# Another order of a pair's jobs on all four engines of an attention and expert kernel

## The chip, the cores and the metric

One core of a Trainium2 chip runs the whole program. The metric is the device time of one execution in microseconds. Three executions of the kernel before took 3823.05, 3824.71 and 3825.47 us; the median is 3824.71 us. Five engines work side by side, each through its own list of instructions in program order, and wait for one another by semaphores: TensorE (PE, with its weight loads PEld), VectorE (DVE), ScalarE (ACT), GpSimd (POOL) and SyncE (SP), which here issues the DMAs.

## The reference

The input x is [8, 512, 256]. After a layer norm two branches are computed and both are added to x.

```python
xn = _layernorm(x, axis=-1)
# branch 1: causal attention, 16 heads of 16
score = einsum('bhqd,bhkd->bhqk', Q, K) / sqrt(16) + causal mask
out1 = (softmax(score) @ V) @ WO
# branch 2: 16 heads of 64, experts E = 8 with the best 2 kept
q = _rope(einsum('bsd,hdp->bhsp', x, Wq));  k = _rope(einsum('bsd,hdp->bhsp', x, Wk))
gv = _gate(x, Wsel_v);  go = _gate(x, Wsel_o)          # sigmoid, top 2 of 8
v = einsum('bsd,bhse,hedp->bhsp', x, gv, Wv)
o = einsum('bhst,bhtp->bhsp', softmax(q k / 8), v)
src2 = einsum('bhsp,bhse,hepd->bsd', o, go, Wo)
src = _ln(src + src2);  out2 = _ln(src + relu(src @ W1 + b1) @ W2 + b2)
return x + out1 + out2
```

## The kernel before

The program has three stages. The first (about 230 us) normalizes the eight batches, computes the gates and stores them. The second, about 3300 us, goes over 64 pairs: a pair is one batch and two neighbouring heads of both branches, with the weights of two heads kept for eight batches in a row. The third (from about 3540 us) does the feed-forward part, the norms and the sum.

A pass of the loop over pairs works on three pairs at once: it computes the attention scores of pair `it` in eight steps, prepares pair `it + 1` (projections, values, rotated heads) and finishes pair `it - 1` (attend, expert products). Even steps handle a 128-row block of the two big heads, odd steps one of the causal heads. Per step TensorE computes the scores of the next step into two banks (L718, or L723 and L724), then the jobs that a table names for this step, then the transposes of this step's exponentials (L748). VectorE takes the row maxima (L1184), ScalarE the exponentials (L1016) and later copies the transposes out (L1030).

The tables are `PE_FILL`, `ACT_FILL`, `DVE_FILL` and `POOL_FILL`, one list of jobs per step, written out by hand. There is no scheduler: each engine's order is the order of its table, and every wait is computed from the tables. The jobs:

- R, AT, AC: transposed reciprocals (L793), attend (L811) and causal attend (L821) of the pair before; ON on VectorE normalizes the result (L1232).
- U, UH, UL, J, one for each of eight experts: VectorE multiplies the attended heads with an expert's gate (`uf`, L1239), ScalarE copies the high part (`u_h`, L1062), GpSimd subtracts for the low part (`u_l`, L569), TensorE multiplies with the expert's weights (L836) into two banks that collect all eight. Both `uf`, `u_h` and `u_l` have two buffers: U waits for the UL two before it, UH for the J two before it.
- P, four projections of the next pair (L705 with `wq_h`); ScalarE copies each to `raw` (L1044).
- V, eight value tiles (L705 with `wv_h`); VectorE multiplies by the gates and adds up (L1206, L1208).
- RP, RS, PA, PB, VN, SQ, SK on GpSimd: rotation of the heads and splitting of the causal heads into stacked bf16 parts (L580 to L608). VC and VA copy the values for attend (L560, L565). RD widens reciprocals (L574).
- QK, two groups of head transposes (L775); QH and QL make the high and low parts `q_h`, `k_h` (L1047, ScalarE) and `q_l`, `k_l` (L1218, L1220, VectorE). ST and SO: stack transposes (L784) and their copies (L1050).

AT, AC, P, V and QK write to two banks in turn, in the order of the PE table. A job waits until the reader of the bank's last content has freed it: P2 for the raw copy of P0, V6 for q_l of the first head transposes. That rule is these lines:

```python
W_JOBS = {k: [j for j in fills(k, PE_FILL) if j[0] in ("AT", "AC", "P", "V", "QK")] for k in range(5)}
```

A pass of the loop on TensorE is:

```python
if s < SLOTS - 1:
    scores(s + 1, it)
elif kind != LAST:
    heads_ready()
    scores(0, n)
for job in fill(kind, PE_FILL, s):
    do(job)
turn(s)
```

Scores wait until the exponentials of the step before have been taken from their banks. SyncE loads gates, inputs and weights; its waits are on the fourth and eighth U and on V3 and V7.

Of the kernel before, what the change touches and what calls it, by code (L numbers as in the profile page):

```python
# [9 lines left out]
P, E = 64, 8  # L10
# [24 lines left out]
AHEAD = ("P", "V", "QK", "ST", "QH", "QL", "SO", "RP", "RS", "PA", "PB", "VN", "SQ", "SK")  # L35

PE_FILL = [[("R", 0), ("AT", 0), ("AC", 0)],
           [("P", 0), ("P", 1), ("P", 2), ("P", 3)],
           [("J", 0), ("V", 0), ("V", 1)],
           [("J", 1), ("V", 2), ("J", 2)],  # L40
           [("V", 3), ("J", 3), ("V", 4)],
           [("J", 4), ("V", 5), ("J", 5)],
           [("QK", 0), ("QK", 1), ("V", 6), ("J", 6)],
           [("ST", 0), ("ST", 1), ("V", 7), ("J", 7)]]
ACT_FILL = [[("AT", 0), ("AC", 0)],
            [("UH", 0), ("P", 0), ("P", 1), ("UH", 1), ("P", 2), ("P", 3)],
            [("UH", 2)],
            [("UH", 3)],
            [("UH", 4), ("UH", 5)],
            [("UH", 6)],  # L50
            [("QH", 0), ("QH", 1), ("UH", 7)],
            [("SO", 0), ("SO", 1)]]
DVE_FILL = [[("ON", 0), ("U", 0)],
            [("U", 1)],
            [("V", 0), ("U", 2), ("V", 1)],
            [("V", 2), ("U", 3)],
            [("V", 3), ("U", 4), ("U", 5), ("V", 4)],
            [("V", 5), ("U", 6)],
            [("QL", 0), ("QL", 1), ("U", 7), ("V", 6), ("RECIP", 0)],
            [("V", 7), ("YA", 0)]]  # L60
POOL_FILL = [[],
             [("VC", 0), ("VA", 0), ("UL", 0), ("UL", 1)],
             [("RP", 0), ("UL", 2)],
             [("RS", 0), ("UL", 3), ("PA", 0)],
             [("PB", 0), ("UL", 4), ("UL", 5)],
             [("SQ", 0), ("UL", 6)],
             [("VN", 0), ("SK", 0), ("UL", 7)],
             [("RD", 0)]]
V_ORDER = [(0, 0), (0, 1), (1, 0), (1, 1), (0, 2), (0, 3), (1, 2), (1, 3)]

# [10 lines left out]
def fill(kind, table, s):  # L81

    return [j for j in table[s] if present(kind, j)]


def fills(kind, table):

    return [j for s in range(SLOTS) for j in fill(kind, table, s)]
# [42 lines left out]
def build(nc, x, wqk, wv, wo, wsel, w_out, w1, w2, b1, rows, ident, ident_h, mask, rope, rank, out):  # L131
# [12 lines left out]
    with ExitStack() as ctx:  # L144
# [819 lines left out]
        def _(act):  # L964
# [45 lines left out]
            def exps(s, n):  # L1010

                qt, w = s // 2, S if s % 2 == 0 else (s // 2 + 1) * NP
                for j in range(2):
                    act.wait_ge(nmax_ready, n * UNITS + 2 * s + j + 1)
                    kw = {"accum_out": den[:, qt, j:j + 1]} if s % 2 == 0 else {}
                    nc.scalar.activation(probs[:, s % 2, j, 0:w], sbank[j][:, 0:w], ACT.Exp, bias=nmax[:, 2 * s + j:2 * s + j + 1], **kw).then_inc(exp_done, 1)  # L1016

            def body(kind, it):
# [19 lines left out]
                def do(job):  # L1038
                    name, i = job
                    if name == "P":  # L1040
                        o, free = w_filled(job)
                        if i == 0 and kind != PRO:
                            act.wait_ge(stack_ready, n)
                        nc.scalar.activation(raw[:, i, :], o[:, 0:NPROJ], ACT.Copy).then_inc(free, 1)  # L1044
                    elif name == "QH":
                        o, _ = w_filled(("QK", i))
                        nc.scalar.activation((q_h, k_h)[i][:], o[:], ACT.Copy, scale=(P ** -0.5, 1.0)[i]).then_inc(qk_high, 1)  # L1047
                    elif name == "SO":
                        act.wait_ge(t_full[i], t_at(kind, it, i, ("ST", i)) + 1)
                        nc.scalar.activation(stackT[:, 2 * i:2 * i + 2, :], tbank[i].bitcast(bf16)[0:STK, :].rearrange("q (g s) -> q g s", g=2),  # L1050
                                             ACT.Copy, scale=(CA ** -0.5, 1.0)[i]).then_inc(t_free[i], 1)
                    elif name == "AT":
                        o, free = w_filled(job)
                        nc.scalar.activation(oo[:, 0], o[:], ACT.Copy).then_inc(free, 1)
                    elif name == "AC":
                        o, free = w_filled(job)
                        act.wait_ge(a_stored, 64 * of + 16)
                        nc.scalar.activation(a_out[:], o[0:2 * STRIP, :], ACT.Copy).then_inc(free, 1)
                    else:
                        act.wait_ge(u_ready, of * E + i + 1)  # L1060
                        act.wait_ge(o_done, of * E + i - 1) if kind == TAIL or i > 1 else None
                        nc.scalar.activation(u_h[:, i % 2], uf[:, i % 2], ACT.Copy).then_inc(uh_done, 1)  # L1062

                if kind in (PRO, TAIL):
                    for job in fills(kind, ACT_FILL):
                        do(job)
# [3 lines left out]
                for s in range(SLOTS):  # L1070
                    if s < SLOTS - 1:
                        exps(s + 1, it)
                    elif kind != LAST:
                        exps(0, n)
                    for job in fill(kind, ACT_FILL, s):
                        do(job)
# [29 lines left out]
        def _(dve):  # L1106
# [72 lines left out]
            def row_max(s, n):  # L1179

                w = S if s % 2 == 0 else (s // 2 + 1) * NP
                for j in range(2):
                    dve.wait_ge(s_full, n * UNITS + 2 * s + j + 1)
                    nc.vector.tensor_reduce(nmax[:, 2 * s + j:2 * s + j + 1], sbank[j][:, 0:w], AX.X, ALU.max, negate=True).then_inc(nmax_ready, 1)  # L1184

            def body(kind, it):
# [61 lines left out]
                if kind in (PRO, TAIL):  # L1248
                    for job in fills(kind, DVE_FILL):
                        do(job)  # L1250
# [3 lines left out]
                for s in range(SLOTS):  # L1254
                    if s < SLOTS - 1:
                        row_max(s + 1, it)
                    elif kind != LAST:
                        row_max(0, n)
                    for job in fill(kind, DVE_FILL, s):
                        do(job)  # L1260
# [100 lines left out]
```

## Time and profile before

| what | value |
|---|---|
| median of 3 executions | 3824.71 us |
| the profiled execution's own time | 3826.32 us |
| its span, first to last instruction | 3824.5 us |
| busy: TensorE, VectorE, ScalarE, GpSimd | 3358.3, 2142.5, 1823.2, 1722.9 us |
| mean granted TensorE clock | 0.97 of 2.4 GHz |
| moved by DMA | 265.57 MB, 69 GB/s over the span |

Busy time of one engine overlaps that of the others, so the shares don't add up. A row of the timeline gives the start of a group of like instructions, its length, and in square brackets how long the engine had been idle before it and whose work ended the idle time. The chain of waits follows the work that ended last back from step to step; a row there gives start, length and what ran. In a row "x6" is the count of instructions.

### The profile page before, as it was taken

The page shows a single profiled execution, that of the slowest core. Times are in us where ns is not written, and L with a number is a line of the kernel's source. Part 1 is how long each engine was busy: PE and PEld are TensorE (multiplying, and loading weights), DVE is VectorE, ACT ScalarE, POOL GpSimd, SP SyncE. Part 2 cuts the span into 40 slices and gives each one's busy share as a digit, 9 for nine tenths or more (in the row PEclk, how much of TensorE's full clock was granted, in tenths as well). Part 3 has the DMA queues.
Part 4 walks back from the last instruction along what each step waited for, and adds up shares of the span by engine and source line. Part 5 has one row for each costly group of instructions (what it writes and reads, how often), then busy time and mean ns, then how long its engine had stood idle before and what let it go on. Part 6 is the DMA issues. An engine that isn't in the chain of part 4 may idle for free.

```text
span 3824.5 us, 63063 instructions
## 1 busy us (share of the span) xinstructions
PE 3358.3 (88%) x18656; PEld 2456.8 (64%) x18656; DVE 2142.5 (56%) x3602; ACT 1823.2 (48%) x3906; POOL 1722.9 (45%) x1911
## 2 busy tenths in 40 slices
PE   2259999999999999999999999999999999998998
PEld 1246666666666666666666666666666666665666
DVE  6765555555555555555555555555555555555553
ACT  2235555555555555555555555555555555554211
POOL 2124445544554455444554465445544455444122
PEclk7679999999999999999999999999999999999999
DMA  3122233222322232223222322222322222223121
GB/s 107 62 87 54 55 83 79 67 63 56 94 59 60 68 82 79 61 58 82 63 68 68 82 77 53 68 61 74 79 68 67 74 71 68 55 65 91 58 66 44
DMA packets 88947, 265.57 MB, mean 69 GB/s; under 512 B 28240, under 2 KB 40784, under 8 KB 72272
## 3 DMA queue, kind: packets, MB, share of 16 engines
q1 hardware_dynamic: 88912, 265.15, 26.5%
q8 instruction: 17, 0.28, 0.0%
q14 instruction: 18, 0.15, 0.0%
HBM read 243.61 MB, written 21.50 MB: 69 GB/s over the span
## 4 chain that ended last, share of the span: by engine, by line
PE 57%; issue 19%; DVE 10%; POOL 8%; ACT 6%; ACTq 0%; DMA 0%; POOLq 0%; SPq 0%; DVEq 0%
PE bank L705 14%; PE bank L836 10%; PE bank L748 6%; PE bank L811 6%; PE bank L718 5%; PE bank L821 4%; PE bank L944 4%; PE bank L936 3%; POOL u_l L569 3%; PE bank L784 2%; ACT raw L1044 1%; ACT pt_c L1030 1%; DVE vm L1206 1%; ACT probs L1016 1%; DVE nmax L1184 1%
## 5 line engine op out<-in xcount | busy, mean ns | idle before, releaser
L569 POOL TENSOR_TENSOR u_l<-uf,u_h 128x512 fp32r<-128x512 f32 x512 | 653.2, 1287 | 1009.6 <-ACT u_h L1062 1009.5
L705 PE MATMUL bank<-wv_h,xx 128*128 128x512 f32 x2048 | 738.3, 407 | 153.2 <-DVE q_l L1218 153.2
L1184 DVE TENSOR_REDUCE nmax<-bank 128x1 f32<-128x512 f32 (+3 forms) x1024 | 556.3, 585 | 518.3 <-PE bank L724 267.4
L1062 ACT ACTIVATE u_h<-uf 128x512 fp32r<-128x512 f32 x512 | 323.7, 633 | 824.7 <-DVE uf L1239 815.3
L1016 ACT ACTIVATE probs<-bank,nmax 128x512 f32<-128x512 f32 (+3 forms) x1024 | 590.5, 607 | 222.3 <-DVE nmax L1184 219.3
L1206 DVE TENSOR_TENSOR vm<-bank,gv 128x512 f32<-128x512 f32 x512 | 353.7, 691 | 536.8 <-PE bank L705 536.8
L705 PEld LDWEIGHTS bank<-wv_h,xx 128*128 128x128 f32 x2048 | 390.5, 191 | 254.9 <-DVE q_l L1218 168.4
L836 PE MATMUL bank<-u_h,wo_h 128*128 128x512 f32 x1024 | 427.5, 417 | 39.3 <-POOL u_l L569 34.2
L748 PE MATMUL bank<-ident_sb,probs 128*128 128x128 f32 x3328 | 456.0, 275 | 0.9 <-ACT stackT L1050 0.9
L748 PEld LDWEIGHTS bank<-ident_sb,probs 128*128 128x128 f32 x3328 | 389.4, 141 | 73.8 <-issue 13.3
L705 PE MATMUL bank<-wv_l,xx 128*128 128x512 f32 x1024 | 406.6, 397 | 0.0
L1239 DVE TENSOR_TENSOR uf<-oo,go 128x512 f32<-128x512 f32 x512 | 396.1, 783 | 17.3 <-POOL u_l L569 8.0
L836 PE MATMUL bank<-u_h,wo_l 128*128 128x512 f32 x1024 | 404.8, 395 | 0.0
L836 PE MATMUL bank<-u_l,wo_h 128*128 128x512 f32 x1024 | 403.5, 394 | 0.0
L1208 DVE TENSOR_REDUCE v_next<-vm 128x64 f32<-128x512 f32 x512 | 351.4, 686 | 17.5
L705 PE MATMUL bank<-wq_h,xx 128*128 128x352 f32 x1024 | 282.3, 338 | 69.6 <-ACT raw L1044 63.3
L1030 ACT ACTIVATE pt_e<-bank 128x512 f32<-128x512 f32 x512 | 275.5, 589 | 126.9 <-PE bank L748 126.7
L560 POOL TENSOR_TENSOR v_sb<-v_next,zero_hb 128x512 f32<-128x512 f32 x64 | 76.6, 1196 | 494.0 <-PE bank L811 488.9
L836 PEld LDWEIGHTS bank<-u_h,wo_h 128*128 128x128 f32 x1024 | 193.9, 189 | 147.7 <-issue 86.2
L705 PEld LDWEIGHTS bank<-wq_h,xx 128*128 128x128 f32 x1024 | 183.5, 190 | 111.0 <-ACT raw L1044 81.5
L811 PE MATMUL bank<-pt_e,v_sb 128*64 128x512 f32 x1024 | 233.8, 598 | 0.0
L836 PEld LDWEIGHTS bank<-u_h,wo_l 128*128 128x128 f32 x1024 | 192.7, 188 | 45.0
(141 smaller groups left out, 5012.0 us busy)
## 6 DMA issues: line engine op xcount, KB each, us to landing
go<-go_d SPq DMA_DIRECT2D x256, 512.0 KB, 6.2
xx<-xs_d SPq DMA_DIRECT2D x128, 512.0 KB, 3.6
pt_c<-in_x SPq DMA_DIRECT2D x16, 512.0 KB, 4.6
st<-in_wv SPq DMA_DIRECT2D x16, 512.0 KB, 6.6
xs_d<-xx SPq DMA_DIRECT2D x8, 1024.0 KB, 4.1
st<-in_wo SPq DMA_DIRECT2D x16, 512.0 KB, 7.4
a_d<-a_out SPq DMA_DIRECT2D x128, 32.0 KB
uf<-a_d SPq DMA_DIRECT2D x16, 256.0 KB
```

What stands on the lines that cost most here:

```text
L569: nc.gpsimd.tensor_tensor(u_l[:, e % 2], uf[:, e % 2], u_h.bitcast(f32)[:, e % 2], ALU.subtract).then_inc(ul_done, 1)
L705: last = nc.tensor.matmul(out, lhs, rhs, start=n == 1, stop=n == 3 * len(chunks))
L748: mm = nc.tensor.transpose(o[:, c * NP:(c + 1) * NP], probs[:, s % 2, j, c * NP:(c + 1) * NP], ident_sb[:])
L811: mm = nc.tensor.matmul(o[j * P:(j + 1) * P, :], v_sb[:, k, j, :], pt_e[:, j, k, :], start=k == 0, stop=k == TT - 1)
L836: mm = nc.tensor.matmul(ybank[i][:], w[:, e, c], u[:, e % 2], start=e == 0 and k == 0, stop=e == E - 1 and k == 2, skip_group_check=True)
L1016: nc.scalar.activation(probs[:, s % 2, j, 0:w], sbank[j][:, 0:w], ACT.Exp, bias=nmax[:, 2 * s + j:2 * s + j + 1], **kw).then_inc(exp_done, 1)
L1030: nc.scalar.activation(dst[:, j, 0:m, qt * NP:(qt + 1) * NP], tbank[j][:, 0:m * NP].rearrange("q (c m) -> q c m", m=NP), ACT.Copy).then_in ...
L1062: nc.scalar.activation(u_h[:, i % 2], uf[:, i % 2], ACT.Copy).then_inc(uh_done, 1)
L1184: nc.vector.tensor_reduce(nmax[:, 2 * s + j:2 * s + j + 1], sbank[j][:, 0:w], AX.X, ALU.max, negate=True).then_inc(nmax_ready, 1)
L1206: nc.vector.tensor_tensor(m, o[:].rearrange("q (c e) -> q c e", e=E), g, ALU.mult).then_inc(free, 1)
L1208: nc.vector.tensor_reduce(v_next[:, t, j, :], m, AX.X, ALU.add).then_inc(v_ready, 1)
L1239: nc.vector.tensor_tensor(uf[:, i % 2], oo[:, 1], go[:, i], ALU.mult).then_inc(u_ready, 1)
```

## The change

The four tables are rewritten; nothing else is. Each job is done as often as before, by the same engine, with the same waits. Three things move. The first expert product stands between the projections P1 and P2 (the first two `u_h` and U come in the first step for it), and from there expert products and value tiles alternate. The two head transposes stand at the end of the sixth step instead of the start of the seventh, with QH and QL to match, and UH and U of the eighth expert come ahead of them. On GpSimd and VectorE u work comes a little earlier among the other jobs. The steps are counted from one.

```diff
 PE_FILL = [[("R", 0), ("AT", 0), ("AC", 0)],
-           [("P", 0), ("P", 1), ("P", 2), ("P", 3)],
-           [("J", 0), ("V", 0), ("V", 1)],
-           [("J", 1), ("V", 2), ("J", 2)],
-           [("V", 3), ("J", 3), ("V", 4)],
-           [("J", 4), ("V", 5), ("J", 5)],
-           [("QK", 0), ("QK", 1), ("V", 6), ("J", 6)],
+           [("P", 0), ("P", 1), ("J", 0), ("P", 2), ("P", 3)],
+           [("V", 0), ("J", 1), ("V", 1)],
+           [("V", 2), ("J", 2), ("V", 3)],
+           [("J", 3), ("V", 4), ("J", 4)],
+           [("V", 5), ("J", 5), ("QK", 0), ("QK", 1)],
+           [("J", 6), ("V", 6)],
            [("ST", 0), ("ST", 1), ("V", 7), ("J", 7)]]
-ACT_FILL = [[("AT", 0), ("AC", 0)],
-            [("UH", 0), ("P", 0), ("P", 1), ("UH", 1), ("P", 2), ("P", 3)],
-            [("UH", 2)],
+ACT_FILL = [[("AT", 0), ("AC", 0), ("UH", 0), ("UH", 1)],
+            [("P", 0), ("P", 1), ("UH", 2), ("P", 2), ("P", 3)],
             [("UH", 3)],
-            [("UH", 4), ("UH", 5)],
-            [("UH", 6)],
-            [("QH", 0), ("QH", 1), ("UH", 7)],
+            [("UH", 4)],
+            [("UH", 5), ("UH", 6)],
+            [("UH", 7), ("QH", 0), ("QH", 1)],
+            [],
             [("SO", 0), ("SO", 1)]]
-DVE_FILL = [[("ON", 0), ("U", 0)],
-            [("U", 1)],
-            [("V", 0), ("U", 2), ("V", 1)],
-            [("V", 2), ("U", 3)],
-            [("V", 3), ("U", 4), ("U", 5), ("V", 4)],
-            [("V", 5), ("U", 6)],
-            [("QL", 0), ("QL", 1), ("U", 7), ("V", 6), ("RECIP", 0)],
+DVE_FILL = [[("ON", 0), ("U", 0), ("U", 1)],
+            [("U", 2)],
+            [("V", 0), ("U", 3), ("V", 1)],
+            [("V", 2), ("U", 4), ("V", 3)],
+            [("U", 5), ("V", 4), ("U", 6)],
+            [("V", 5), ("U", 7), ("QL", 0), ("QL", 1)],
+            [("V", 6), ("RECIP", 0)],
             [("V", 7), ("YA", 0)]]
 POOL_FILL = [[],
              [("VC", 0), ("VA", 0), ("UL", 0), ("UL", 1)],
-             [("RP", 0), ("UL", 2)],
-             [("RS", 0), ("UL", 3), ("PA", 0)],
-             [("PB", 0), ("UL", 4), ("UL", 5)],
-             [("SQ", 0), ("UL", 6)],
-             [("VN", 0), ("SK", 0), ("UL", 7)],
+             [("UL", 2), ("RP", 0), ("UL", 3)],
+             [("RS", 0), ("UL", 4)],
+             [("PA", 0), ("UL", 5), ("PB", 0)],
+             [("UL", 6), ("SQ", 0)],
+             [("UL", 7), ("VN", 0), ("SK", 0)],
              [("RD", 0)]]
```

Below are two places in the instruction lists, in program order without times. REGISTER_ALU and ISA rows only prepare or hold a wait.

On TensorE, second step of a pass, between the second projection and the third (L705 with wq), the difference of the two orders:

```order
 L705 MATMUL bank<-wq_l,xx 128x352
 L705 MATMUL bank<-wq_h,xx 128x352
+L827 ISA
+L832 ISA
+L836 MATMUL bank<-u_h,wo_h 128x512
+L836 MATMUL bank<-u_l,wo_h 128x512
+L836 MATMUL bank<-u_h,wo_l 128x512
+L836 MATMUL bank<-u_h,wo_h 128x512
+L836 MATMUL bank<-u_l,wo_h 128x512
+L836 MATMUL bank<-u_h,wo_l 128x512
 L734 REGISTER_ALU
 L705 MATMUL bank<-wq_h,xx 128x352
```

The six matmuls of the first expert product (L836) now stand between the two projections; they stood behind the next scores.

On TensorE, before, the head transposes (L775) and what stands on either side: scores of the causal heads ahead, the value tile V6 and an expert product behind.

```order
L723 MATMUL bank<-stackT 128x512
L724 MATMUL bank<-mask_sb,ident_hb 128x128
L734 REGISTER_ALU
L773 REGISTER_ALU
L775 MATMUL bank<-ident_sb,raw 128x128 x8
L734 REGISTER_ALU
L705 MATMUL bank<-wv_h,xx 128x512
L705 MATMUL bank<-wv_l,xx 128x512
L705 MATMUL bank<-wv_h,xx 128x512 x2
L705 MATMUL bank<-wv_l,xx 128x512
L705 MATMUL bank<-wv_h,xx 128x512
```

The same place on TensorE in the changed kernel, from the head transposes on:

```order
L775 MATMUL bank<-ident_sb,raw 128x128 x8
L739 REGISTER_ALU
L746 REGISTER_ALU
L748 MATMUL bank<-ident_sb,probs 128x128 x3
L739 REGISTER_ALU
L748 MATMUL bank<-ident_sb,probs 128x128 x3
L712 REGISTER_ALU
L723 MATMUL bank<-stackT 128x512
L724 MATMUL bank<-mask_sb,ident_hb 128x128
L723 MATMUL bank<-stackT 128x512
L724 MATMUL bank<-mask_sb,ident_hb 128x128
L827 REGISTER_ALU
```

Behind the last row come the six matmuls of the seventh expert product and only then V6: six transposes, the scores and a product now lie between the head transposes and the tile that reuses their bank.

On ScalarE, before, around the copies of the turned heads (q_h, k_h):

```order
L1030 ACTIVATE pt_c<-bank 128x3x128
L1029 REGISTER_ALU
L1030 ACTIVATE pt_c<-bank 128x3x128
L1016 ACTIVATE probs<-bank,nmax 128x512 x2
L1035 REGISTER_ALU
L1047 ACTIVATE q_h<-bank 128x512
L1035 REGISTER_ALU
L1047 ACTIVATE k_h<-bank 128x512
L1060 REGISTER_ALU
L1062 ACTIVATE u_h<-uf 128x512
```

And in the changed kernel:

```order
L1062 ACTIVATE u_h<-uf 128x512
L1035 REGISTER_ALU
L1047 ACTIVATE q_h<-bank 128x512
L1035 REGISTER_ALU
L1047 ACTIVATE k_h<-bank 128x512
L1029 REGISTER_ALU
L1030 ACTIVATE pt_c<-bank 128x3x128
L1029 REGISTER_ALU
L1030 ACTIVATE pt_c<-bank 128x3x128
L1016 ACTIVATE probs<-bank,nmax 128x512 x2
```

q_h and k_h have moved ahead of the pt_c copies and the exponentials of the eighth step, and the last u_h has moved ahead of q_h.

## Rows read from the trace of the kernel before

**Rows 1.** The page, busy time of each engine over the span.
```profile
PE 3358.3 (88%) x18656; PEld 2456.8 (64%) x18656; DVE 2142.5 (56%) x3602; ACT 1823.2 (48%) x3906; POOL 1722.9 (45%) x1911
```

**Rows 2.** Waits of TensorE, 400 to 3400 us: total us, times, longest.
```profile
PE bank L705 <- DVE q_l L1218: 140.4, 58, 2.4
PE bank L705 <- ACT raw L1044: 59.9, 59, 1.0
PE bank L836 <- POOL u_l L569: 29.8, 59, 0.5
```

**Rows 3.** Chain of waits, pieces in order: start us, us, what.
```profile
298.10 3.58 PE bank L811 x16
...
1527.69 3.58 PE bank L811 x16
...
1556.14 1.39 PE bank L705 x6
...
1568.15 1.65 PE bank L705 x6
...
1578.66 1.43 PE bank L811 x5
...
3473.79 3.58 PE bank L811 x16
```

**Rows 4.** Chain of waits in another pair, 590 to 612 us.
```profile
595.28 2.93 PE bank L705 x6
```

**Rows 5.** Windows: us, busy of PE, PEld, DVE, ACT, POOL; clock, DMA share, GB/s.
```profile
1527.70:1578.70 51.00, 47.02 (x274) 34.55 (x276) 28.52 (x47) 26.70 (x59) 25.83 (x30) 1.00 0.26 63
595.00:598.50 3.50, 3.22 (x8) 2.60 (x9) 1.68 (x4) 0.63 (x1) 1.34 (x2) 0.55 0.27 89
3560.00:3800.00 240.00, 239.18 (x923) 165.78 (x922) 125.96 (x329) 49.38 (x86) 51.19 (x21) 1.00 0.19 60
```

**Rows 6.** Timeline of TensorE in one pair, around its three waits.
```profile
1537.29 0.32 PE L705 MATMUL bank<-wq_h,xx 128*128 128x352 f32 x1
1538.60 0.43 PE L705 MATMUL bank<-wq_h,xx 128*128 128x352 f32 x1 [1.00 <-ACT raw L1044]
...
1554.52 0.47 PE L836 MATMUL bank<-u_h,wo_h 128*128 128x512 f32 x1 [0.51 <-POOL u_l L569]
...
1564.70 1.04 PE L775 MATMUL bank<-ident_sb,raw 128*128 128x128 f32 x8
1568.15 0.50 PE L705 MATMUL bank<-wv_h,xx 128*128 128x512 f32 x1 [2.41 <-DVE q_l L1218]
```

**Rows 7.** Timeline of ScalarE in the same pair.
```profile
1534.28 1.06 ACT L1030 ACTIVATE pt_e<-bank 128x512 f32<-128x512 f32 x2
1538.09 0.81 ACT L1044 ACTIVATE raw<-bank 128x352 f32<-128x352 f32 x2
...
1566.76 0.61 ACT L1047 ACTIVATE q_h<-bank 128x512 fp32r<-128x512 f32 x1
```

**Rows 8.** Timeline of VectorE in the same pair.
```profile
1532.89 0.69 DVE L1239 TENSOR_TENSOR uf<-oo,go 128x512 f32<-128x512 f32 x1
...
1556.23 1.16 DVE L1239 TENSOR_TENSOR uf<-oo,go 128x512 f32<-128x512 f32 x1
...
1562.30 0.69 DVE L1206 TENSOR_TENSOR vm<-bank,gv 128x512 f32<-128x512 f32 x1 [1.67 <-PE bank L705]
...
1563.63 0.68 DVE L1239 TENSOR_TENSOR uf<-oo,go 128x512 f32<-128x512 f32 x1
...
1567.41 0.69 DVE L1218 SCALAR_TENSOR_TENSOR q_l<-bank,q_h 128x512 fp32r<-128x512 f32 x1 [1.50 <-ACT q_h L1047]
```

**Rows 9.** Timeline of GpSimd in the same pair.
```profile
1533.72 0.43 POOL L565 TENSOR_TENSOR va<-va_next,zero_hb 128x128 f32<-128x128 f32 x1 [1.11 <-PE bank L821]
...
1547.18 1.29 POOL L569 TENSOR_TENSOR u_l<-uf,u_h 128x512 fp32r<-128x512 f32 x1 [2.89 <-ACT u_h L1062]
...
1555.83 1.01 POOL L594 TENSOR_TENSOR part<-rot,zero_hb 128x256 bf16<-128x256 f32 x1
```

## The prediction

> **What bounds the kernel now.** I read the page first: TensorE is busy 88% of the span, VectorE 56%, the others under 50% [rows 1]. So TensorE sets the pace, and the question is what stands in its idle time. The list of waits gives that for the long loop over pairs: between 400 and 3400 us, in 59 pairs, it waits 140.4 us for q_l of VectorE, 59.9 us for the copy raw of ScalarE and 29.8 us for u_l of GpSimd, and for nothing else [rows 2]. The chain of waits gives a pair's length: the attend product starts at 298.10 and 3473.79 us with 62 pairs between, and from 1527.69 to the next at 1578.66 in an ordinary one, 50.97 us [rows 3]. In that pair TensorE is busy 47.0 of 51.0 us [rows 5]. About 4 us of each pair can be won, and no more, as no product is removed.
>
> Some pairs are longer. In one of them the value tile behind the q_l wait takes 2.93 us instead of 1.65, and the granted clock around it is 0.55, so part of it ran at the lower level of 1.2 GHz [rows 3 to 5]; the chain has nine such rows in the loop, 1.28 us each. With 3175.69 us for the 62 pairs and 62 times 50.97 being 3160.1, 15.6 us remain, of which they are 11.5.
>
> **What each wait really costs.** The idle time is counted from a matmul's end, which lies behind its issue, and the first matmul after a wait takes longer to make room. By starts [rows 6]: eight head transposes start at 1564.70 and take 0.96 us to issue, the value product behind them starts at 1568.15, so 2.49 us; its first start-to-start is 0.34 and not 0.23, so 2.6. The second projection's last matmul starts at 1537.29 and the third projection at 1538.60; a matmul of that size takes 0.16 to issue, so 1.15, with its slow first 1.26. Before the fourth expert product at 1554.52 the idle time shown is 0.51; with the same 0.16 and the slow first it is 0.75. Together 4.6 us a pair, of which 3.9 show as idle.
>
> **The change, part by part.** Nothing is added or removed on any engine; the order alone moves. I follow one pair with the old durations, time 0 being the start of the attend product. Issue times on TensorE [rows 3, 6]: attend 3.58, causal attend until 5.9 (its reader starts at 6.03, [rows 9]), value tile 1.39 and expert product the same (six matmuls of 512 columns both), projection 6 times 0.16 and its start, 1.02, eight transposes 0.96, even scores 0.9, odd ones 0.3 to 0.56. I add 0.1 for an expert product that follows scores.
> New order: causal 3.6, transposes 5.9, scores 6.8, projections P0 7.7 and P1 8.7, product J0 9.8, P2 11.25, P3 12.3, value V0 13.8, J1 15.2, V1 16.6, V2 19.9, J2 21.3, V3 22.7, J3 25.0, V4 26.5, J4 27.9, V5 31.1, J5 32.5, head transposes 33.9, scores 35.5, J6 36.1, V6 37.6, transposes 39.0, next scores 39.9, stack transposes 40.8, V7 41.7, J7 43.2, next attend 46.5.
> Now each thing that could be late.
>
> First product before P2. On ScalarE the first two u_h copies now stand ahead of the pt_e copies, which started at 6.6 [rows 7]; uf is written at 5.2 to 5.9 and the next behind it [rows 8], so the copies run 6.6 to 7.6 and pt_e to 8.7. GpSimd has va until 6.5 [rows 9], then u_l in 1.29 us [rows 9] from 7.2: done at 8.5, where J0 wants it at 9.8. Cost nothing; the cover is P0 and P1. The exponentials slip from 8.5 to 8.75, and the raw copy of P0, which waited behind them and one u_h and started at 10.4 [rows 7], starts at 10.1 and ends at 10.6. P2 wants that at 11.25: the 1.15 us wait goes, because J0's 1.4 us stand where it was. Slack 0.65 us.
>
> Expert products alternate with value tiles. u is now one step further ahead: with the waits in force (a u needs the u_l two before it, a u_h the product two before it) u_l of J1 is done at 9.8 (wanted 15.2), of J2 at 13.4 (21.3), of J3 at 19.5 (25.0), of J4 at 25.5 (27.9), of J5 at 29.3 (32.5), of J6 at 32.6 (36.1), of J7 at 36.8 (43.2). The 0.68 us wait goes, the nearest next one has 2.4 us left.
>
> Head transposes at the end of the sixth step. They need the rotation, done near 21, and the banks of V4 and V5, the latter free at 33.4 for a second group that starts at 34.4. Behind them stand six transposes, the scores and J6, together 2.7 us of work where there was none. The chain to V6 is: V5 done on TensorE, its two VectorE passes (1.33 from the first to the u behind them), u 0.69, a copy 0.53 from start to start, q_h 0.61, q_l 0.69 [rows 7, 8]: q_l ends at 36.7, V6 wants it at 37.6. Slack 0.9 us, though U7 and its copy are now ahead of q_h and q_l. k_l and the row maxima follow, the exponentials end at 39.2, the next scores want them at 39.9. Slack 0.7 us, the tightest but one. On GpSimd the stack copies end near 38.5, wanted at 40.8.
>
> Queues. SyncE's order is unchanged; its loads wait for the fourth and eighth u and for V3 and V7, which all come earlier in the pair, and their data are wanted half a pair later. Once per eight pairs GpSimd splits the next value weights at the end of a pair: two halves of two passes over 1024 elements, each at most twice the 1.29 us of u_l's 512 [rows 9]. From 42.7 on that is 10.3 us, until 6.5 of the next pair; v_sb, another 1.3, and va 0.43 follow, u_l then ends at 9.5. J0 still wants it at 9.8: cost nothing, with 0.3 us to spare.
>
> **GpSimd and VectorE together.** A u took 1.16 us instead of 0.68 beside GpSimd's part split, and the split itself took 1.0 [rows 8, 9]. In the new order the third and the seventh u lie beside GpSimd work. I took 0.4 us more for each; their u_l have over 3 us left, so this costs 0. The least is 0, the most is all eight u's at 0.48, 3.8 us on VectorE, which has 22 us idle in a pair: it would eat the 0.7 and 0.9 us slacks and add under 1 us a pair. I take 0, since the row shows it for two u's of eight.
>
> **Sum.** A pair is shorter by 4.6 less 0.15 for the new starts behind a wait, 4.45 us; 62 pairs give 276 us. The slow clock comes right behind the 2.4 us wait, which goes: 12 us more. The first pair (without products, its waits partly stay) gives 1 us, a guess; the last pair and the closing stage are taken as they are. 289 us from the profiled execution's own 3826.3 us leave 3537 us. The median shown is 1.6 us below the own time, less than the estimate's error; I stay at 3537. The bounds of this case: if all 4.6 us and the whole 15.6 us go, 3826 less 301, so 3525; if only the idle seen is won, 3.92 by 62, and the clock dips stay, 3583.
>
> **Rivals.**
> (A) The clock dips stay. They cost 1.28 us in nine of the pairs. For it: transposes and short scores still stand in a row in steps six and seven. Against: the dips I see all begin at the matmul after the 2.4 us idle, and between 3560 and 3800 us TensorE is busy 239 of 240 us at clock 1.00 [rows 5]. Time 3537 plus 12, so 3549. The Trainium skill (TensorE: Matmul & The Clock Gate, Part 4: PE-mode transpose) says that transposes do not count as busy for the clock gate as other matmuls do; by that rule 14 transposes in a row could be read as a pause. The rows at 595 us show a dip behind transposes and a wait together, so they do not separate the two.
> (B) A new wait takes part of the gain. The three tight places are P2 on raw (0.65 us left), V6 on q_l (0.9) and the scores on the exponentials (0.7); all hang on ScalarE doing in order what it did later before. One being 1 to 2 us later than I put it costs 0.3 to 1.3 us in each of 62 pairs: 19 to 80 us, middle 50, so 3587. For it: four engines in fixed order, and the contention above. Against: each chain is short and made of durations that hardly vary.
> (C) Slower than before: U7 and its copy stand ahead of q_h on ScalarE and q_l on VectorE, and U7 waits for the sixth u_l. A u_l later than 34.1, where U7 could start, holds up V6, all that follows and the next pair. The sixth u_l, at 29.3 in my walk, would have to be 4.8 us late to show, 0.9 more to reach V6 and another 4.45 to make the pair longer than before: it decides from 10.2 us late. At 12 us late a pair is 1.8 us longer and the kernel takes 3826 plus 112, 3938. Against: nothing in GpSimd's queue before it is 10 us long; it has 25.8 us of work in the pair [rows 5].
> (D) The waits change names and the pair stays at 51 us: 3825. It would take a wait outside TensorE's banks, and none of the other engines is over 29 us busy in a pair [rows 5].
>
> **Chances.** Forecast 0.66, (A) 0.09, (B) 0.20, (C) 0.03, (D) 0.02. A difference of 0.2%, about 8 us, is what a measurement can tell here. Faster: 0.95; within: 0.02; slower: 0.03. The forecast's own range is 3522 to 3583; with (A) inside it and most of (B), 3520 to 3605 leaves out about 0.15.
>
> **What would show it.** In the new profile: attend to attend 46.4 to 46.7 us; TensorE busy 94% or more; no wait for q_l or raw, none for u_l above 0.3 us; the third projection starting right behind a product; the granted clock without single dips in the loop; the raw copy of the first projection ending before the first expert product does. If the pair is 47 to 48 us, the wait that ends last in it, before P2, V6 or the scores, names which slack I got wrong. If all 62 are 46.5 us and the time still misses, the first or last pairs or the closing stage moved, which I left alone.

## The result: 8.1% faster, and beyond the forecast's range

The changed kernel takes 3513.02 us (median of 4, 3512.62 to 3513.2) against 3825.04 us (3823.05 to 3825.47). The ratio is 0.9186, 95% interval 0.9175 to 0.9198. I had forecast 3537 us with a range of 3520 to 3605: the direction and the mechanism held, the gain of 312 us is 24 us more than I gave, and 7 us beyond the range's lower end.

Page of the changed kernel, busy time of each engine, answers to [rows 1]:

```profile
PE 3296.6 (94%) x18656; PEld 2453.1 (70%) x18656; DVE 2160.5 (62%) x3602; ACT 1841.1 (52%) x3906; POOL 1728.1 (49%) x1911
```

TensorE does the same 18656 matmuls in 62 us less busy time (less low clock, and no matmul that runs out ahead of a wait or starts slowly behind one) and stands idle 252 us less. The list of TensorE's waits between 400 and 3100 us, which had three rows in [rows 2], is empty. The window there (columns as in [rows 5]):

```profile
400.00:3100.00 2700.00, 2696.61 (x15842) 2018.06 (x15841) 1680.72 (x2683) 1567.89 (x3377) 1497.68 (x1703) 1.00 0.30 77
```

3.4 us idle in 2700. The loop is bound by TensorE's own work now. The attend products in the chain of waits, first, two in the middle, last two:

```profile
292.12 3.58 PE bank L811 x16
...
1496.86 3.58 PE bank L811 x16
1543.21 3.58 PE bank L811 x16
...
3164.72 3.58 PE bank L811 x16
3194.69 3.61 PE bank L811 x16
```

62 pairs take 2872.60 us, 46.33 each, against 3175.69 [rows 3]. Every pair is between 46.3 and 46.4 us. So the 313.7 us by which the span is shorter are: 303.1 in the 62 pairs, 6.0 ahead of the first attend product (298.10 to 292.12), 6.0 in the last pair (35.98 to 29.97), and 1.4 lost behind it.

TensorE's timeline of one pair at the three former waits, answers to [rows 6]:

```profile
1506.46 0.33 PE L705 MATMUL bank<-wq_h,xx 128*128 128x352 f32 x1
1506.62 0.40 PE L836 MATMUL bank<-u_h,wo_h 128*128 128x512 f32 x1
...
1508.02 0.32 PE L705 MATMUL bank<-wq_h,xx 128*128 128x352 f32 x1
...
1530.66 1.04 PE L775 MATMUL bank<-ident_sb,raw 128*128 128x128 f32 x8
...
1534.19 0.39 PE L705 MATMUL bank<-wv_h,xx 128*128 128x512 f32 x1
```

No row has a bracket with idle time, and the third projection's first matmul takes 0.32 instead of 0.43. The other engines in the same pair (ScalarE, then VectorE, then GpSimd), answers to [rows 7 to 9]:

```profile
1506.77 0.81 ACT L1044 ACTIVATE raw<-bank 128x352 f32<-128x352 f32 x2
...
1532.05 0.58 ACT L1047 ACTIVATE q_h<-bank 128x512 fp32r<-128x512 f32 x1
```

```profile
1505.88 1.36 DVE L1239 TENSOR_TENSOR uf<-oo,go 128x512 f32<-128x512 f32 x1
...
1532.65 0.69 DVE L1218 SCALAR_TENSOR_TENSOR q_l<-bank,q_h 128x512 fp32r<-128x512 f32 x1 [1.18 <-ACT q_h L1047]
```

```profile
1502.90 0.75 POOL L565 TENSOR_TENSOR va<-va_next,zero_hb 128x128 f32<-128x128 f32 x1 [1.11 <-PE bank L821]
1504.15 2.54 POOL L569 TENSOR_TENSOR u_l<-uf,u_h 128x512 fp32r<-128x512 f32 x2 [0.50 <-ACT u_h L1062]
```

q_l ends at 1533.34 (1532.65 and 0.69), V6 starts at 1534.19: 0.85 us of slack, where the walk had 0.9. The first of the two raw copies ends near 1507.2 (one takes 0.47), the third projection starts at 1508.02: 0.8, where it had 0.65. Counted from the attend product's first matmul at 1496.79, J0 stands at 9.8 and V6 at 37.4 us; the walk had 9.8 and 37.6.

### The profile page after: what moved, and what is told of

Same layout as the page of the kernel before. It is cut to its first block, busy times and chain, and to the rows that moved or that the text cites. A ratio compares the mean times of both kernels' runs of the same rounds, so it can differ in the third digit from the quotient of the medians.

```text
span 3510.8 us, 63063 instructions
## 1 busy us (share of the span) xinstructions
PE 3296.6 (94%) x18656; PEld 2453.1 (70%) x18656; DVE 2160.5 (62%) x3602; ACT 1841.1 (52%) x3906; POOL 1728.1 (49%) x1911
## 4 chain that ended last, share of the span: by engine, by line
PE 93%; DVE 5%; issue 1%; ACT 1%; DMA 0%; POOL 0%; SPq 0%; POOLq 0%; DVEq 0%; ACTq 0%
PE bank L705 28%; PE bank L836 20%; PE bank L748 11%; PE bank L811 7%; PE bank L718 7%; PE bank L821 4%; PE bank L944 4%; PE bank L936 3%; PE bank L723 2%; PE bank L784 2%; PE bank L775 2%; PE bank L679 1%; PE bank L724 1%; PE bank L793 1%; DVE pt_e L1161 1%
## 5 line engine op out<-in xcount | busy, mean ns | idle before, releaser
L705 PE MATMUL bank<-wv_h,xx 128*128 128x512 f32 x2048 | 743.3, 404 | 0.7 <-DVE q_l L1218 0.7
L1062 ACT ACTIVATE u_h<-uf 128x512 fp32r<-128x512 f32 x512 | 316.4, 629 | 531.2 <-DVE uf L1239 480.0
L705 PEld LDWEIGHTS bank<-wv_h,xx 128*128 128x128 f32 x2048 | 384.7, 188 | 125.5 <-issue 46.2
L1239 DVE TENSOR_TENSOR uf<-oo,go 128x512 f32<-128x512 f32 x512 | 414.8, 821 | 17.8 <-POOL u_l L569 8.5
L836 PE MATMUL bank<-u_h,wo_h 128*128 128x512 f32 x1024 | 414.8, 405 | 5.4 <-ACT u_h L1062 2.6
L836 PE MATMUL bank<-u_h,wo_l 128*128 128x512 f32 x1024 | 405.0, 396 | 0.0
L836 PE MATMUL bank<-u_l,wo_h 128*128 128x512 f32 x1024 | 403.4, 394 | 0.0
L705 PE MATMUL bank<-wv_l,xx 128*128 128x512 f32 x1024 | 401.4, 392 | 0.0
L705 PE MATMUL bank<-wq_h,xx 128*128 128x352 f32 x1024 | 275.6, 332 | 6.1 <-DMA xx<-xs_d 6.1
L836 PEld LDWEIGHTS bank<-u_h,wo_h 128*128 128x128 f32 x1024 | 192.8, 188 | 55.2 <-issue 5.2
L836 PEld LDWEIGHTS bank<-u_h,wo_l 128*128 128x128 f32 x1024 | 192.4, 188 | 44.6
L836 PEld LDWEIGHTS bank<-u_l,wo_h 128*128 128x128 f32 x1024 | 193.2, 189 | 37.0
```

The lines of the kernel that those rows point to most:

```text
L705: last = nc.tensor.matmul(out, lhs, rhs, start=n == 1, stop=n == 3 * len(chunks))
L836: mm = nc.tensor.matmul(ybank[i][:], w[:, e, c], u[:, e % 2], start=e == 0 and k == 0, stop=e == E - 1 and k == 2, skip_group_check=True)
L1239: nc.vector.tensor_tensor(uf[:, i % 2], oo[:, 1], go[:, i], ALU.mult).then_inc(u_ready, 1)
```

## Experiments

Two theories stood at the start. W: each of the three waits has its price in issue gaps (2.6, 1.26 and 0.75 us a pair), and the prices add up. I: a wait is worth only the idle time that the list shows. After the first runs a third question took over, about the low clock.

**One part at a time, from the kernel before.**

j0_only:
```diff
-           [("P", 0), ("P", 1), ("P", 2), ("P", 3)],
-           [("J", 0), ("V", 0), ("V", 1)],
+           [("P", 0), ("P", 1), ("J", 0), ("P", 2), ("P", 3)],
+           [("V", 0), ("V", 1)],
...
-ACT_FILL = [[("AT", 0), ("AC", 0)],
-            [("UH", 0), ("P", 0), ("P", 1), ("UH", 1), ("P", 2), ("P", 3)],
+ACT_FILL = [[("AT", 0), ("AC", 0), ("UH", 0)],
+            [("P", 0), ("P", 1), ("UH", 1), ("P", 2), ("P", 3)],
```


> The kernel before with one thing changed: the first expert product stands between the second and the third projection (its u_h comes in the first step for it). Theory W (each of TensorE's three waits costs the gap between the issues around it plus the slow first matmul, 1.26 us here): a pair 49.71 us, 78 us less in 62 pairs, 3747 us; the wait for raw is gone, q_l and u_l waits stay, and so do the single slow-clock intervals behind the q_l wait. Rival I (a wait costs only the idle time the list of waits shows, 1.00 us here, and the rest of the gain came from elsewhere): 3763 us. Rival S (the parts only work together): the raw wait comes back in another place and the time stays at 3825 us.

Measured 3822.08 us, ratio 0.9995 (0.9984 to 1.0006): nothing. Waits of TensorE between 450 and 3100 us:

```profile
PE bank L705 <- DVE q_l L1218: 125.7, 52, 2.4
PE bank L836 <- POOL u_l L569: 26.3, 52, 0.5
```

The raw wait is gone as W says. But the chain of waits shows this in two pairs that follow each other, and 61 of the 62 pairs are like them:

```profile
1524.41 3.58 PE bank L811 x16
...
1563.59 2.93 PE bank L705 x6
1575.59 3.58 PE bank L811 x16
...
1614.80 2.92 PE bank L705 x6
```

The value tile behind the q_l wait takes 2.93 us, the low clock's length of [rows 4], in all pairs but one. In the kernel before it was ten of the 62, not nine as I had counted: the first pair of the loop has a low interval too (52.62 us long). A pair is 51.18 us, the one clean pair 49.76. All three theories missed that: W's 1.26 us were won (50.97 to 49.76) and 1.4 us of low clock came in for them. The window from 450 to 3100 us shows a granted clock of 0.97, where the kernel before has 0.99:

```profile
450.00:3100.00 2650.00, 2496.73 (x14073) 1844.28 (x14070) 1474.01 (x2380) 1378.28 (x3003) 1336.71 (x1520) 0.97 0.27 70
```

The last pair fell from 35.98 to 32.20 us by this part alone.

heads_only:
```diff
-           [("J", 4), ("V", 5), ("J", 5)],
-           [("QK", 0), ("QK", 1), ("V", 6), ("J", 6)],
+           [("J", 4), ("V", 5), ("J", 5), ("QK", 0), ("QK", 1)],
+           [("V", 6), ("J", 6)],
...
-            [("UH", 6)],
-            [("QH", 0), ("QH", 1), ("UH", 7)],
+            [("UH", 6), ("QH", 0), ("QH", 1)],
+            [("UH", 7)],
```
(QL and U7 on VectorE likewise.)

> The kernel before with one thing changed: the two head transposes end the sixth step, with their q_h, k_h and q_l, k_l copies; V6 stands before J6 as it did. Six transposes and the scores, 1.2 us, now cover part of the wait. Theory W: q_h still follows the seventh u_h, so 0.3 to 0.5 us of idle time stays for q_l; the pair 48.9 us, 127 us less plus 12 us for the slow-clock intervals that go: 3686 us. Rival I: only 2.0 us less idle, 3701 us, slow-clock intervals in the loop as before. Rival S: 3825 us.

Measured 3692.03 us, 0.9655 (0.9627 to 0.9683). The q_l wait falls to 0.5 us a pair and the loop has no low interval; a pair is 49.09 us. That is 6 us above W: the wait left is at the top of what I gave, and the pair 0.2 us longer than W had. The first attend product starts 4 us earlier than before, which hides part of that.

swap_only:
```diff
-           [("QK", 0), ("QK", 1), ("V", 6), ("J", 6)],
+           [("QK", 0), ("QK", 1), ("J", 6), ("V", 6)],
```


> The kernel before with one thing changed: in the seventh step the expert product J6 stands before the value tile V6, which waits for q_l. Theory W: V6 starts when q_l ends as before, and J6's 1.4 us are done by then, so the pair is 1.4 us shorter, 86 us; the idle in one piece falls from 2.4 to under 1 us. If the slow clock follows that idle, its intervals go too: 3727 us. Rival C (the slow clock follows the row of transposes and short matmuls, not the idle time): they stay, 3739 us. Rival S: the u_l of J6 becomes the wait and nothing is won, 3825 us.

Measured 3727.82 us, 0.9748 (0.972 to 0.9777), and no low interval in the loop: W within 1 us. The 62 pairs gave 96.1 of W's 98 us; that the total fits closer is chance, since the first projection started 2.1 us earlier in this run. One swapped entry of one table is worth 97 us. What is left of the long wait is 0.7 us of idle time in front of J6 (for u_l) and 0.2 us in front of V6. The transposes and scores stand in a row as before, which speaks against rival C.

alternation_only:
```diff
-           [("J", 0), ("V", 0), ("V", 1)],
-           [("J", 1), ("V", 2), ("J", 2)],
-           [("V", 3), ("J", 3), ("V", 4)],
-           [("J", 4), ("V", 5), ("J", 5)],
+           [("J", 0), ("V", 0), ("J", 1), ("V", 1)],
+           [("V", 2), ("J", 2), ("V", 3)],
+           [("J", 3), ("V", 4), ("J", 4)],
+           [("V", 5), ("J", 5)],
```
(U and UH of the middle steps move to match; GpSimd's table is the one of the change.)

> The changed kernel with the first expert product put back behind the fourth projection and the head transposes back in the seventh step: only the alternation of expert products and value tiles, and u earlier, are left of the change. Theory W: the u_l wait (0.75 us) goes, q_l and raw waits stay: 50.2 us a pair, 46 us less, 3779 us; slow-clock intervals stay. Rival I: 0.51 us a pair, 3793 us. In the last pair, where TensorE waits for the expert chain, this part alone gives up to the 6 us that the whole change gave there (theory); the rival is that those 6 us came with the first product.

Measured 3824.48 us, 1.0001 (0.999 to 1.0012): nothing again, though the u_l wait is gone. From the chain of waits, three pairs, the first two with a slow value tile, the third without:

```profile
913.45 3.58 PE bank L811 x16
...
952.99 2.91 PE bank L705 x6
965.05 3.58 PE bank L811 x16
...
1004.52 2.92 PE bank L705 x6
1016.43 3.58 PE bank L811 x16
...
1066.44 3.58 PE bank L811 x15
```

51.60, 51.38 and 50.01 us. Of 62 pairs 48 are above 51.3 and 14 near 50.0 or 50.3. A clean pair is 0.7 to 1.0 us shorter than the 50.97 before, so W's 0.75 was there, and the low clock took it. The last pair did not gain here (37.48 us), as the rival has it. Of the last pair's 6.0 us, j0_only alone gives 3.8.

**Is it the idle time that brings the low clock?** j0_only is the place to ask, since it has it in every pair. Two kernels fill the wait for q_l with work that is thrown away:

```diff
                         turn_heads(i)
+                        if i == 1 and kind == INNER:
+                            o = t_bank(0, ("turn", 6))
+                            for m in range(20):
+                                nc.tensor.transpose(o[:, (m % 4) * NP:(m % 4 + 1) * NP], ident_sb[:], ident_sb[:])
```
(fill_transposes; fill_matmuls has nine matmuls of `xx` with `wv_h` in their place.)

> j0_only (the kernel before with the first expert product between the second and third projection, 51.2 us a pair, the low clock level in every pair) with nine more matmuls of 512 columns behind the head transposes, 2.2 us of work into a transpose bank that is overwritten later; their result is not used. V6 still waits for q_l, so they take no time of their own. Theory (the low level follows the idle time in front of V6): no low intervals, 49.8 us a pair, 87 us less than j0_only, 3735 us. Rival (the low level comes with the pair's length or with the row of transposes and scores before the wait, whatever fills it): 3822 us or more.

> As fill_matmuls, but the 2.2 us are filled with twenty transposes of 128 columns, whose result is not used. Theory (idle time alone counts, transposes are work like any other): as fill_matmuls, 3735 us and no low intervals. Rival (transposes do not count as work for the clock, which is what the Trainium skill says in TensorE: Matmul & The Clock Gate, Part 4: PE-mode transpose): low intervals as in j0_only, 3822 us.

Measured 3728.06 us (0.9747, 0.9718 to 0.9775) and 3727.07 us (0.9744, 0.9716 to 0.9772). Both are 94 and 95 us faster than j0_only, with more work per pair. The timeline of fill_transposes at the place:

```profile
1524.80 1.04 PE L775 MATMUL bank<-ident_sb,raw 128*128 128x128 f32 x8
1525.68 2.35 PE L851 MATMUL bank<-ident_sb 128*128 128x128 f32 x20
1528.25 0.50 PE L705 MATMUL bank<-wv_h,xx 128*128 128x512 f32 x1 [0.23 <-DVE q_l L1222]
```

V6 waits for q_l still, 0.23 us. No pair has the low clock: all 62 are between 49.6 and 49.9 us, in both kernels, and the window shows 1.00 where j0_only had 0.97:

```profile
450.00:3100.00 2650.00, 2608.63 (x15575) 1956.96 (x15572) 1520.65 (x2452) 1421.78 (x3097) 1383.52 (x1565) 1.00 0.28 72
```

A clean pair of j0_only was as long (49.76 us), and the transposes and scores ahead of the wait are the same. So the low clock needs the idle time, here 2.4 us; the pair's length or what stands before the wait do not bring it by themselves. And the twenty float32 transposes kept the clock high as well as the nine matmuls did. The rule of the Trainium skill (TensorE: Matmul & The Clock Gate, Part 4: PE-mode transpose) that transposes do not count the same way is not borne out at this place; the trace calls them MATMUL like all others and doesn't show which mode they ran in. This is the one experiment that shows directly that the low clock needs the idle time.

**One part undone, from the changed kernel.**

heads_back:
```diff
-           [("V", 5), ("J", 5), ("QK", 0), ("QK", 1)],
-           [("J", 6), ("V", 6)],
+           [("V", 5), ("J", 5)],
+           [("QK", 0), ("QK", 1), ("V", 6), ("J", 6)],
...
-            [("UH", 7), ("QH", 0), ("QH", 1)],
             [],
+            [("QH", 0), ("QH", 1), ("UH", 7)],
```
(QL and U7 on VectorE likewise.)

> The changed kernel with one thing undone: the head transposes and their copies are back in the seventh step, V6 ahead of J6. Theory W: TensorE waits 2.4 us for q_l again, 2.6 us a pair, 48.9 us, plus 161 us: 3674 us where the clock stays high. Theory L (learned from the first four runs: with the q_l wait in place the low clock level comes in many pairs and costs 1.4 us each, and how many depends on where the wait falls): between 3674 and 3761 us, with low intervals in the loop. Rival: without the other two waits the low level stays rare as in the kernel before: 3674 to 3685 us.

Measured 3715.95 us, 0.9717 (0.9698 to 0.9737). Waits of TensorE, 450 to 3100 us, and the window:

```profile
PE bank L705 <- DVE q_l L1218: 114.3, 53, 2.2
```

```profile
450.00:3100.00 2650.00, 2530.60 (x14560) 1881.21 (x14558) 1556.46 (x2463) 1444.97 (x3106) 1390.78 (x1570) 0.98 0.28 72
```

31 of the 62 pairs are 48.6 to 49.0 us and 31 are 50.2 to 50.5. In 29 of the long ones the record of the granted clock has a low interval, so nearly every second pair; the other two, the 7th and the 15th, have none, and TensorE stands idle 1.2 us ahead of an expert product there, which no other pair shows and which I did not follow up. That is theory L, whose range was wide (87 us); W and the rival lie 31 to 42 us too low. The head transposes' place is worth 203 us beside the other parts, against 133 us alone, and some 45 us of that are the low clock's (29 times 1.54, the difference of the two kinds of pair).

j0_back, then j0_back2, which also moves the third u_h:
```diff
-           [("P", 0), ("P", 1), ("J", 0), ("P", 2), ("P", 3)],
-           [("V", 0), ("J", 1), ("V", 1)],
+           [("P", 0), ("P", 1), ("P", 2), ("P", 3)],
+           [("J", 0), ("V", 0), ("J", 1), ("V", 1)],
...
-            [("P", 0), ("P", 1), ("UH", 2), ("P", 2), ("P", 3)],
-            [("UH", 3)],
+            [("P", 0), ("P", 1), ("P", 2), ("P", 3)],
+            [("UH", 2), ("UH", 3)],
```
(The first hunk is j0_back, both are j0_back2.)

> The changed kernel with one thing undone: the first expert product stands behind the fourth projection again (ahead of V0), the u_h copies stay early. Theory W: the copy raw of the first projection ends at 10.45 us after the attend product's start, the third projection wants it at 9.8: 0.6 us idle, 0.75 us in all, pair 47.1 us, 3559 us, clock high throughout. Rival I: 0.6 us a pair, 3550 us. Rival C (any wait behind a row of products brings the low level back): above 3590 us.

> As j0_back, with the third u_h moved behind the raw copies of the third and fourth projection on ScalarE too, where j0_back left it ahead of them and so made V0 wait for the first expert product. Theory W: one wait of 0.6 us is left, ahead of the third projection, 0.75 us in all: 47.1 us a pair, 3559 us. Rival: both waits come from the place of the product itself and the pair stays at 48.5 us, 3653 us.

j0_back measured 3652.67 us, 0.9552 (0.9533 to 0.9571), 94 us above what W said. The clock is high throughout; TensorE waits twice a pair:

```profile
PE bank L705 <- ACT raw L1044: 92.8, 109, 1.1
```

109 times in 55 pairs: 0.5 us ahead of the third projection and 1.1 us ahead of the value tile V0. The third u_h waits for the first product, which now stands behind the fourth projection, and it is ahead of the raw copies of the third and fourth projection on ScalarE. So those copies come late, and V0, which writes to the third projection's bank, waits. My edit had moved only one of two places that belong together. j0_back2 measured 3567.41 us, 0.9327 (0.9299 to 0.9354), one wait a pair (31.7 us, 56 times), most pairs 47.1 us. W to 8 us. Seven pairs, every eighth, are 47.6 us. heads_only, swap_only and j0_back have such a pair 0.2 to 0.4 us longer every eighth time too, the changed kernel has none. Weights are kept for eight pairs in a row, so their split is the likely cause; no run tests it.

v6_first:
```diff
-           [("J", 6), ("V", 6)],
+           [("V", 6), ("J", 6)],
```


> The changed kernel with V6 ahead of J6 in the seventh step. q_l ends 36.55 us after the attend product's start; V6 would start at 35.9. Theory W: 0.65 us idle and a slow first matmul, 0.75 us a pair, 46 us, 3559 us, clock high. Rival (J6's place is free, as q_l has 0.85 us of slack): 3513 us.

Measured 3555.37 us, 0.9295 (0.9268 to 0.9322), a wait for q_l of 0.5 us, a pair of 47.02. J6's place is worth 42 us beside the other parts.

**How much room is left on the path to V6.** delay1 and delay4 put one and four ScalarE copies ahead of q_h:
```diff
+                        for m in range(4 if i == 0 and kind == INNER else 0):
+                            nc.scalar.activation(spare[:, m], zero_hb[:], ACT.Copy)
                         nc.scalar.activation((q_h, k_h)[i][:], o[:], ACT.Copy, scale=(P ** -0.5, 1.0)[i]).then_inc(qk_high, 1)
```


> The changed kernel with one more ScalarE copy of 512 columns (about 0.53 us) ahead of q_h in every pair; its result is not used. In the trace of the changed kernel q_l ends 0.85 us before V6 starts, and the exponentials end 0.66 us before the scores that reuse their bank. Theory: the delay is inside both, 3513 us, within 3 us. Rival B (no slack: what delays q_l delays the pair): 33 us more, 3546 us.

> The changed kernel with four more ScalarE copies (about 2.1 us) ahead of q_h in every pair; their results are not used. Theory: 2.1 less the 0.85 us of slack is 1.3 us idle before V6, 1.5 us a pair with the slow first matmul, 93 us more, 3606 us. If an idle time of 1.3 us is enough for the low clock level, another 1.4 us in some pairs: up to 3693 us; if it takes the 2.4 us of the kernel before, no low intervals in the loop.

delay1: 3513.11 us, 0.9187 (0.9171 to 0.9202), the changed kernel's time. delay4: 3606.19 us, 0.943 (0.9412 to 0.9449). Its wait and its window:

```profile
PE bank L706 <- DVE q_l L1221: 61.9, 55, 1.1
```

```profile
450.00:3100.00 2650.00, 2581.30 (x15055) 1917.10 (x15054) 1589.42 (x2551) 1595.63 (x3430) 1434.70 (x1624) 1.00 0.29 75
```

Both as the theory had it: one copy stays inside the slack of 0.85 us, and four (2.1 us) make a pair 1.52 us longer where the theory had 1.5. An idle time of 1.1 us in every pair leaves the clock at 1.00. No run here has a single wait between 1.1 and 2.2 us in the loop.

## Why the prediction was right in kind and off in size

**What bounds the kernel, and the three waits.** Right. TensorE set the pace, its three waits were the gain, and no fourth wait took their place.

**What each wait costs.** Right with 4.6 us a pair, and wrong where the sum took 0.15 off again "for the new starts behind a wait". An ordinary pair went from 50.97 to 46.33, 4.64 us: TensorE doesn't wait any more, so no start pays for a wait. 4.64 less the 4.45 of the sum is 0.19 us, by 62 pairs 12 us of the miss.

**First product, alternation, head transposes, slacks.** Right. The walk's starts agree with the trace of the pair shown to 0.2 us. delay1 and delay4 put the slack to V6 between one copy and four and fit 0.9 us. That two parts alone returned nothing, the walk did not foresee; more on this below.

**Contention between VectorE and GpSimd.** In the pair shown the third u takes 1.36 us beside GpSimd's u_l, the sixth 0.94 and the seventh 0.75 instead of 0.68, 1.0 us more in all where I gave 0.4 each to the third and the seventh. va takes 0.75 instead of 0.43 us. Over the changed kernel's trace the 193 u's that lie more than half beside GpSimd work take 0.96 us on average, the 225 beside none 0.68. It stays within the slack and costs nothing, as forecast.

**The first and the last pair.** This step failed: the sum gave 1 us to the first pair, a guess, and took the last pair and the closing stage "as they are". The two ends gave 12. The last pair, windows of the kernel before and of the changed one, and the two long waits in it before:

```profile
3473.79:3509.77 35.98, 30.78 (x168) 20.48 (x170) 15.26 (x26) 20.78 (x46) 12.72 (x11) 0.95 0.26 60
3164.72:3194.69 29.97, 28.78 (x169) 19.13 (x170) 15.77 (x26) 20.55 (x46) 13.08 (x11) 1.00 0.35 77
```

```profile
3483.83 0.28 PE L723 MATMUL bank<-stackT 96*128 96x256 bf16 x1 [1.90 <-ACT probs L1016]
3485.75 0.70 PE L836 MATMUL bank<-u_h,wo_h 128*128 128x512 f32 x1 [1.40 <-ACT u_h L1062]
```

No projections are left to work on there, so TensorE waits for the exponentials and the expert chain. TensorE's idle time fell by 4.0 us (35.98 less 30.78, against 29.97 less 28.78), and its busy time by 2.0: a low interval, which stood behind these two waits, is gone. j0_only shows that the first product's place, with its u_h, makes 3.8 of the 6.0 us (32.20 us, without a low interval too).

Ahead of the first attend product, 2.3 of the 6.0 us are that the first projection starts at 234.72 instead of 237.03 us. The change doesn't touch that: the other runs have it anywhere from 234.4 to 236.9, so it is luck. The other 3.7 are mostly the first q_l wait and the slow tile behind it. The 1.4 us lost behind the last attend product are of the same kind as the 2.3; the runs have 314.8 to 316.4 us there.

So the miss adds up, from the profiled executions: 313.7 us against a forecast of 289. In the 62 pairs 303.1 against 288 (of these 15 us, 12 come from the 0.19 us a pair above and 3 to 4 from the low clock), at the two ends 12.0 against 1, and 1.4 lost behind them: 24.7 us.

**The low clock.** Right that it came behind the 2.4 us wait and would go with it, too small by 3 to 4 us, and wrong in what it is tied to. The pairs before were 15.6 us longer than 62 ordinary ones, all of it went, and I had counted nine rows with 12; there were ten long pairs, at 1.39 us 13.9 of the 15.6. I took its number for fixed as long as the wait is there. It isn't: with a wait of 2.4 us in every pair it came in 10 of 62 pairs in the kernel before and in 61 of 62 in j0_only, with one of 2.2 us in 48 in alternation_only and in 29 in heads_back. The change without the head transposes is forecast by my steps at 124 us of gain. heads_back is that kernel and gained 109 us, while j0_only and alternation_only gained none each.

What picks the pairs stays open. The record of the granted clock has one more sign: counted from the attend product, the low interval starts at 41.0, 40.6, 40.3, 39.9 and 39.6 us in the first five pairs of alternation_only, the sixth has none, and then come 40.3, 40.0 and 39.6, where the wait ends near 39.6 in each. In j0_only it starts at 39.1 to 39.2 us in all 61 pairs that have it. So its start can drift against the pair and is not set by the wait's end alone; no run tests what it follows.

**Rivals.** A, B, C and D did not come. My range's lower end was drawn from the loop alone, with the ends left at zero. The loop gave 303 us where that end allowed 301; the ends' 12 us, less the 1.4 behind them, are what put the time outside.

## What to carry to other kernels

Read the bound engine's waits by issue gaps and add first-matmul costs, and give the ends of a loop their own walk, since where fewer jobs run another chain is the path. Before testing a reorder in parts, look whether a long TensorE wait brings the low clock: while one such wait is left, taking out others can return nothing, as it did twice here. Filling the wait with work that is thrown away tells in one run whether it does.

## What the runs showed of the hardware

In the loop the granted clock fell to its lower level of 1.2 GHz only in kernels where TensorE waited 2.2 to 2.4 us in every pair, at a price of 1.4 us each (49.76 to 51.18 us a pair). It stayed at 2.4 GHz in the loop of every kernel whose waits were 1.1 us or less. In the last pair before it fell behind two shorter waits close together, 1.90 and 1.40 us, so 2.2 us in one piece is not a lower bound. How many of the long waits in the loop were followed by it differed: 10, 29, 48 or 61 of 62. What picks them was not tried. Twenty float32 transposes of the identity kept the clock up as nine matmuls of 512 columns did (3727.07 and 3728.06 us).
